# A graph layer and a feed-forward layer on one core: the node pass written out straight, its up product in three single-pass products, its first statistics on ScalarE, and smaller rings in the edge pass

## The reference

```python
def reference(x, src, dst, W, attn_l, attn_r, W_res, W1, b1, W2, b2, ...):
    h = layernorm(x)
    hv = h.reshape(n, 12, 64)
    ft = einsum('nhd,od->nho', hv, W)                  # per head, one 64x64 matrix
    e = leaky_relu(sum(ft * attn_l)[src] + sum(ft * attn_r)[dst], 0.2)
    alpha = segment_softmax(e, dst)
    agg = segment_sum(alpha[:, :, None] * ft[src], dst, n)
    res = einsum('nhd,od->nho', hv, W_res)
    x = x + relu(agg + res)
    t = layernorm(x)
    # rows 6 and up: one hidden layer of 96; the first 6 rows: pairs of experts and a gate
    x = x + concat(class_rows(t[:6]), gelu(t[6:] @ W1 + b1) @ W2 + b2)
    return x
```

## Time and profile before

| | us |
|---|---|
| median of three runs | 3060.57 |
| the profiled execution, its own time | 3053.38 |
| its span, first to last instruction | 3051.6 |
| TensorE busy | 2867.4 (94%) |
| VectorE busy | 2484.8 (81%) |
| GpSimd busy | 2140.6 (70%) |
| ScalarE busy | 1829.4 (60%) |

### The profile page before, as it was taken

The page is one execution under the profiler, slowest core; times in us unless marked ns, Lnnn a source line. Parts: engine busy times, 40 slices in busy tenths (PEclk is TensorE's granted clock), DMA queues, the critical chain, the costliest instruction groups (busy, mean ns, idle before and its releaser), DMA issues. The chain is left out here.

```text
span 3051.6 us, 69396 instructions
## 1 busy us (share of the span) xinstructions
PE 2867.4 (94%) x20124; PEld 2554.1 (84%) x20124; DVE 2484.8 (81%) x5828; ACT 1829.4 (60%) x3384; POOL 2140.6 (70%) x2027
## 2 busy tenths in 40 slices
PE   2999999999999984799999999999999999999998
PEld 2988888888888863688888888898988989889896
DVE  4799999999999964688878787787877888778883
ACT  1666666666666631566666666666666666666662
POOL 6766666666666500778877787787877878778782
PEclk9999999999999995799999999999999999999998
DMA  7999999988888624799988888888888888888873
GB/s 180 203 223 217 215 214 224 214 218 218 217 216 217 175 90 156 237 325 315 317 287 309 272 300 286 287 298 287 295 286 276 299 275 301 272 276 295 277 253 122
DMA packets 246672, 758.47 MB, mean 249 GB/s; under 512 B 78899, under 2 KB 81203, under 8 KB 246291
## 3 DMA queue, kind: packets, MB, share of 16 engines
q1 hardware_dynamic: 176644, 545.08, 50.4%
q0 software_dynamic: 69312, 209.33, 30.4%
q10 hardware_dynamic: 432, 0.62, 0.1%
HBM read 623.04 MB, written 232.17 MB: 280 GB/s over the span
## 5 line engine op out<-in xcount | busy, mean ns | idle before, releaser
L647 ACT ACTIVATE arena<-ps 128x768 f32<-128x768 f32 x392 | 317.3, 810 | 550.1 <-PE ps L707 550.0
L860 PE MATMUL ps<-wr_bd,arena 128*128 128x128 f32 x4704 | 600.3, 278 | 35.2 <-DVE arena L1179 34.1
L860 PEld LDWEIGHTS ps<-wr_bd,arena 128*128 128x128 f32 x4704 | 565.6, 194 | 43.2 <-issue 34.8
L839 PE MATMUL ps<-arena,w_sb 128*96 128x256 f32 x2352 | 580.6, 383 | 0.0
L570 POOL DMA_INDIRECT arena<-agg_scratch,nrow x392 | 438.9, 1120 | 78.1 <-issue 69.8
L1174 DVE SCALAR_TENSOR_TENSOR ps<-ps,r_n,arena 128x768 f32<-128x768 f32 x392 | 400.1, 1021 | 54.1 <-DMA arena<-agg_scratch,nrow 32.5
L839 PEld LDWEIGHTS ps<-arena,w_sb 128*96 128x96 f32 x2352 | 368.0, 165 | 85.9
L550 POOL TENSOR_SCALAR arena<-csr_neg,mv,r_n 128x768 f32<-128x768 f32 x392 | 385.9, 984 | 52.4 <-POOL r_n L578 42.1
L609 ACT ACTIVATE arena<-ps 128x512 f32<-128x512 f32 x588 | 307.5, 594 | 189.9 <-PE ps L724 188.5
L1163 DVE TENSOR_TENSOR arena<-arena,ps 128x768 f32<-128x768 f32 x392 | 363.7, 928 | 53.3 <-issue 36.5
L1179 DVE SCALAR_TENSOR_TENSOR arena<-ps,arena 128x768 f32<-128x768 f32 x392 | 375.4, 958 | 17.1
(11 more groups left out here) (197 smaller groups left out, 5420.0 us busy)
## 6 DMA issues: line engine op xcount, KB each, us to landing
arena<-in_x SPq DMA_DIRECT2D x196, 768.0 KB, 6.2
arena<-in_x_cols SPq DMA_DIRECT2D x392, 384.0 KB, 4.7
out<-arena SPq DMA_DIRECT2D x195, 768.0 KB, 5.2
agg_scratch<-arena SPq DMA_DIRECT2D x196, 384.0 KB, 6.4
arena<-in_x,e_slot POOLq DMA_INDIRECT x392, 6.5
arena<-agg_scratch,nrow POOLq DMA_INDIRECT x392, 6.2
row_scratch<-e_slot POOLq DMA_INDIRECT x196
nrow<-row_scratch SPq DMA_DIRECT2D x196, 1.0 KB, 7.1
```

The lines of the kernel that those rows point to most:

```text
L839: last = nc.tensor.matmul(ps[0:HID, 6 + v, 0:PAIR * P], w1_sb[:, i, :], t2[:, v, i, :], start=(i == 0), stop=(i == NC - 1))
L860: last = nc.tensor.matmul(pair(1)[:, i * P:(i + 1) * P], xt_ring[:, g, i * P:(i + 1) * P], wr_bd[:], start=True, stop=True)
```

## The change

- Node pass: `U` becomes 196, so the 392 units are two blocks, both written out, and `turns` makes no loop.
- Up product: w1 is split once into w1_hi and w1_lo (float32r). ScalarE's copy writes t2_hi; VectorE makes t2_lo, transposes less t2_hi, in each unit, after L1179 and ahead of ve_n. L839 becomes three products for each of the three before. The next unit's transposes wait for t2_lo and not for the copy.
- First norm: bn_stats and bn_aggr on VectorE and their small operation go; ScalarE makes sum and square for both tiles of a pair, in every unit, linked by one semaphore s_st1.
- Edge pass: the transpose of dst_slot and the comparison move from 9 to 20 chunks behind (`L_DT`), after the transposes of the rows in TensorE's order; the mask ring has 2 places. dst_slot and same_x are copied 15 behind, ahead of the two norm steps of VectorE. `agg_ring` has 2 places (`AR`).
- The copy for the class rows reads PSUM; w1_sb and v_sb move into the arena.

```diff
-U = 28
+U = 196
+AR = 2
+L_DT = 20
@@ turns
-    with eng.Fori(2, n) as b:
-        yield b
+    if n > 2:
+        with eng.Fori(2, n) as b:
+            yield b
@@ tensors
-        mask_ring = part(32424, BODY, P)
-        both_t = part(34216, 2, 2 * D)
-        agg_ring = part(37544, G, D)
+        mask_ring = part(32424, 2, P)
+        both_t = part(32680, 2, 2 * D)
+        agg_ring = part(35752, AR, D)
-        t2 = part(38400, 2, NC, PAIR * P)
+        w1_hi = sb("w1_hi", [P, NC, HID], f32r)
+        w1_lo = sb("w1_lo", [P, NC, HID], f32r)
+        t2_hi = sb("t2_hi", [P, 2, NC, PAIR * P], f32r)
+        t2_lo = sb("t2_lo", [P, 2, NC, PAIR * P], f32r)
@@ ScalarE, node pass
-                    if u % PAIR == 0 and exists(ts, NT):
+                    if exists(ts, NT):
...
-                        act.wait_ge(s_sum1, b * (U // PAIR) + (u - 1) // PAIR + 1)
-                        nc.scalar.activation(junk[:, 0, :], x_ring[:, v, :], ACT.Square, bias=mv1[:, w, 2:3],
-                                             scale=-1.0, accum_out=q_st[:, w, 0:1]).then_inc(s_sq1, 1)
+                        act.wait_ge(s_st1, 2 * t - 1)
+                        nc.scalar.activation(junk[:, 0, :], x_ring[:, v, :], ACT.Square, bias=mv1[:, w, 2 * k:2 * k + 1],
+                                             scale=-1.0, accum_out=q_st[:, w, k:k + 1]).then_inc(s_st1, 1)
...
-                        nc.scalar.activation(t2[:, v, :, k * P:(k + 1) * P], pair(0).rearrange("p (c n) -> p c n", c=NC),
-                                             ACT.Copy).then_inc(s_te2, 1)
+                        nc.scalar.activation(t2_hi[:, v, :, k * P:(k + 1) * P],
+                                             pair(0).rearrange("p (c n) -> p c n", c=NC), ACT.Copy).then_inc(s_te2, 1)
...
-                    if u % PAIR == 1 and exists(t, NT):
+                    if exists(t, NT):
...
-                        at_least(act, s_sq1, b * (U // PAIR) + u // PAIR)
+                        at_least(act, s_st1, 2 * t)
                         at_least(act, s_base, t - XR + 1)
                         nc.scalar.activation(junk[:, 0, :], x_ring[:, v, :], ACT.Copy, scale=1.0 / D,
-                                             accum_out=mv1[:, w, 2:3])\
-                            .then_inc(s_sum1, 1)
+                                             accum_out=mv1[:, w, 2 * k:2 * k + 1])\
+                            .then_inc(s_st1, 1)
@@ TensorE, edge pass
-                    if exists(ct, EC + 1):
-                        at_least(pe, s_mask, ct)
+                    cd = c - L_DT
+                    if exists(cd, EC + 1):
+                        at_least(pe, s_mask, cd)
...
+                    if exists(cd, EC):
+                        v = (i - L_DT) % BODY
+                        pe.wait_ge(s_dsl, 2 * b + (i - L_DT) // G + 1)
+                        nc.tensor.transpose(dst_ps, dst_slot[:, v // G, v % G:v % G + 1].to_broadcast([P, P]), ident[:])\
+                            .then_inc(s_tds, 1)
@@ TensorE, node pass
-                        at_least(pe, s_te2, tt)
+                        at_least(pe, s_lo2, tt)
                         transposes(pair(0), n2[:, (u - L_T2) % 2, :], s_tp2)
...
-                            pe.wait_ge(s_te2, tu + PAIR)
+                            pe.wait_ge(s_lo2, tu + PAIR)
...
-                            last = nc.tensor.matmul(ps[0:HID, 6 + v, 0:PAIR * P], w1_sb[:, i, :], t2[:, v, i, :],
-                                                    start=(i == 0), stop=(i == NC - 1))
+                            for n, (w, h) in enumerate(((w1_hi, t2_hi[:, v]), (w1_lo, t2_hi[:, v]), (w1_hi, t2_lo[:, v]))):
+                                last = nc.tensor.matmul(ps[0:HID, 6 + v, 0:PAIR * P], w[:, i, :], h[:, i, :],
+                                                        start=(i == 0 and n == 0), stop=(i == NC - 1 and n == 2))
@@ VectorE, setup
+            link_up(V.tensor_copy(w1_hi[:], w1_sb))
+            V.tensor_tensor(w1_lo[:], w1_sb, w1_hi[:].bitcast(f32), ALU.subtract)
@@ VectorE, edge pass
+                    gc = 2 * b + (i - 15) // G
+                    if k == 1 and exists(gc, NG):
+                        w = (i - 15) // G % 2
+                        at_least(dve, s_ert, gc - 1)
+                        at_least(dve, s_tds, G * (gc - 1))
+                        V.tensor_copy(dst_slot[:, w, :], dstbf[:, ds(G * gc, G)])
...
-                        at_least(dve, d_agg[j], 16 * (2 * b + (i - L_AGG) // G))
-                        V.scalar_tensor_tensor(agg_ring[:, j, :].rearrange("p (c f) -> p c f", f=P),
+                        at_least(dve, d_agg[v % AR], 16 * (BODY // AR * b + (i - L_AGG) // AR))
+                        V.scalar_tensor_tensor(agg_ring[:, v % AR, :].rearrange("p (c f) -> p c f", f=P),
...
-                    if exists(ct, EC):
-                        v = (i - L_TR) % BODY
+                    cd = c - L_DT
+                    if exists(cd, EC):
+                        v = (i - L_DT) % BODY
                         w, j = v // G, v % G
-                        dve.wait_ge(s_tds, ct + 1)
-                        at_least(dve, s_sum, ct - BODY + 1)
-                        V.tensor_scalar(mask_ring[:, v, :], dst_ps, dst_slot[:, w, j:j + 1], None,
+                        dve.wait_ge(s_tds, cd + 1)
+                        at_least(dve, s_sum, cd - 1)
+                        V.tensor_scalar(mask_ring[:, v % 2, :], dst_ps, dst_slot[:, w, j:j + 1], None,
                                         ALU.is_equal).then_inc(s_mask, 1)
@@ VectorE, node pass
+                    tl = t - L_T2
+                    if exists(tl, NT):
+                        v, k = (u - L_T2) // PAIR % 2, (u - L_T2) % PAIR
+                        f = slice(k * P, (k + 1) * P)
+                        dve.wait_ge(s_te2, tl + 1)
+                        V.tensor_tensor(t2_lo[:, v, :, f], pair(0).rearrange("p (c n) -> p c n", c=NC),
+                                        t2_hi[:, v, :, f].bitcast(f32), ALU.subtract).then_inc(s_lo2, 1)
...
-                        V.tensor_scalar(ve_n[:, w, 0:1], mv1[:, w, 1:2], EPS, None, ALU.add)
-                        V.tensor_scalar(ve_n[:, w, 1:2], q_st[:, w, 0:1], 1.0 / D, EPS, ALU.mult, ALU.add)
+                        V.tensor_scalar(ve_n[:, w, 0:2], q_st[:, w, 0:2], 1.0 / D, EPS, ALU.mult, ALU.add)
...
-                        for h in range(2):
-                            V.bn_stats(bn1[:, u // PAIR % 2, h, :], x_ring[:, v, h * (D // 2):(h + 1) * (D // 2)]).then_inc(s_bn1, 1)
...
-                        V.bn_aggr(mv1[:, w, 0:2], bn1[:, u // PAIR % 2, :, :].rearrange("p a b -> p (a b)")).then_inc(s_ag1, 1)
```

More of the change, by code:

```diff
@@ L146, in gnn_ffn_kernel @@
         n2 = part(32256, 2, D)
-        t2 = part(38400, 2, NC, PAIR * P)
         junk = part(35328, 2, D)
-        cls_x = part(36864, PAIR, D, rows=NCLS // PAIR)
+        cls_x = part(33792, PAIR, D, rows=NCLS // PAIR)
         a1_sb = part(0, NC, NEXP, HID)
@@ L169, in gnn_ffn_kernel @@
         fix_rows = part(25364, 2, D, rows=EH)
-        pens = part(34216, 2, EC, rows=HEADS)
-        m_run = part(34608, EC + 1, rows=HEADS)
-        t_run = part(34806, EC + 1, rows=HEADS)
-        gap = part(35004, 4, EC, rows=HEADS)
-        coef = part(35788, 4, EC, rows=HEADS)
+        pens = part(32680, 2, EC, rows=HEADS)
+        m_run = part(33072, EC + 1, rows=HEADS)
+        t_run = part(33270, EC + 1, rows=HEADS)
+        gap = part(33468, 4, EC, rows=HEADS)
+        coef = part(34252, 4, EC, rows=HEADS)
         w2_sb = part(21504, D, rows=HID + 1)
+        w1_sb = part(24000, NC, HID)
+        v_sb = part(24600, NC * (2 * HEADS + 2))
         w_dup = part(22272, P, rows=DH)
@@ L321, in gnn_ffn_kernel @@
         s_eo = sem("s_eo")
-        d_agg = [sem(f"d_agg{u}") for u in range(G)]
+        d_agg = [sem(f"d_agg{u}") for u in range(AR)]
         d_tab = sem("d_tab")
@@ L342, in gnn_ffn_kernel @@
         d_g = [sem(f"d_g{u}") for u in range(GR)]
-        s_bn1 = sem("s_bn1")
-        s_ag1 = sem("s_ag1")
-        s_sum1 = sem("s_sum1")
-        s_sq1 = sem("s_sq1")
+        s_st1 = sem("s_st1")
+        s_lo2 = sem("s_lo2")
         s_ven = sem("s_ven")
@@ L430, in _ @@
                              tab_d[k * HEADS:(k + 1) * HEADS]).then_inc(l_tab, 16)
-            for u in range(G):
-                sp.wait_ge(d_agg[u], 16 * (EC // G))
+            for u in range(AR):
+                sp.wait_ge(d_agg[u], 16 * (EC // AR))
             sp.dma_start(o_last, tail_v[:, :, P - 1, :]).then_inc(d_last, 16)
@@ L524, in _ @@
                             .then_inc(s_rpd, 1)
-            for u in range(G):
-                pool.wait_ge(d_agg[u], 16 * (EC // G))
+            for u in range(AR):
+                pool.wait_ge(d_agg[u], 16 * (EC // AR))
             pool.wait_ge(s_idx, 1)
@@ L646, in _ @@
                         at_least(act, s_up, b * (U // PAIR) + (u - L_T2) // PAIR - 1)
[L647 to L648 removed]
```

(17 more changed lines are left out.)

63 lines of the change are left out of this document (23 added, 40 removed).

## The result

The changed kernel takes 3024.85 us (median of four runs, 3022.7 to 3033.3) against 3061.51 for the kernel before: ratio 0.9889 [0.9864, 0.9913], 37 us less. The forecast was 74 less. The profiled execution takes 3026.7 us, not 2980, so 47 us have to be found.

The account below looks back on a forecast made before the run. TensorE was taken to bound the kernel, with a gather loop hidden just under it. Straight line -54, node-pass unit -27 and edge pass +8 made -73: profiled 3053.4 to 2980, 7 more for the median, 2987 us; range 2905 to 3075.

Parts of the forecast that it names:

- Straight line, -54: Node pass: writing out both turns removes the loop's instruction waits and low clock, 54 us less.
- TensorE's unit 4.08: Node pass: nine single-pass up products cut TensorE's work per unit from 4.34 to 4.08 us, -102 if all counts.
- VectorE 7.86 a pair: Node pass: t2_lo added and bn work removed take VectorE from 7.43 to 7.86 us a pair, 3.93 a unit.
- The unit T = 4.27, -27 us: Node pass: the odd gather's landing sets the unit at 4.27 us, between bounds 4.08 and 4.50, gaining 27 us.
- 2T = 1.30 + L - 0.86: Node pass: two units span store to gather use, with L the odd gather's landing after the store, 8.1; T = 4.27.
- the one the prediction first wrote: Node pass: loop from ve_n through power, base and odd gather to ve_n two pairs on, 4.30 us a unit before.
- store + 8.1: Node pass: the odd gather lands 8.1 us after the store, when store and the load behind it are through.
- The edge pass, +8: Edge pass: the output ring of two makes chunks wait for stores, between 0 and 18 us, taken as +8.
- The mask's move at 0: Edge pass: moving the mask and its transpose from 9 to 20 chunks behind costs 0.
- The clock: Node pass: TensorE keeps the full clock despite idling some 0.2 us a unit, so nothing was put down.
- Rival 1: Node pass: TensorE stays the bound, the late gather taken up, T = 4.08, -152 us, 2908 us; chance 0.25.
- Rivals 3 and 4: Node pass, gather landing L from issue: 3, L 7.7 to 7.9, about no change, 0.15; 4, 8.1 or more, slower, 0.18.

Follow-up runs that it names:

- the two sides: Kernel before with the node pass written out without a loop, 3013.50 us; changed kernel with the loop put back, 3064.90 us.
- experiment 5: Changed kernel with ve_n put ahead of t2_lo in VectorE's order: 2987.98 us.
- experiments 6 and 7: Changed kernel: 6 with only the even tile of each pair stored, 2953.95 us; 7 with the load of x issued away from the store, 2945.52 us.
- experiment 2: Kernel before with U of 196, so the node pass has no loop, and nothing else: 3013.50 us.
- experiments 1 and 9: 1: kernel before, output ring of two, 3075.56 us; 9: kernel before, mask moved, 3061.87, plus ring of two, 3064.61; changed kernel, ring of three, 3006.97.
- experiment 4: Changed kernel with the up product again in fp32, without w1_hi, w1_lo and t2_lo: 3019.39 us.
- experiment 8: Changed kernel with ve_n ahead of t2_lo and, on GpSimd, each gather issued ahead of n2: 3128.41 us.

## Why the prediction came out wrong

**Direction, and the range of 2905 to 3075, held; the size of the gain did not.** Step by step:

- *Straight line, -54.* Right in kind, a little large: 40 to 50 from the two sides, no "issue" wait of a turn left, and no price for straight code.
- *TensorE's unit 4.08.* Right: 4.10, products at 0.11 to 0.12. As forecast it no longer decides.
- *VectorE 7.86 a pair.* The pair without a late gather is 2013.62 - 2005.48 = 8.14, so 4.07 a unit: h_lo's 0.16 of waiting is in it, and the rest are small differences in start-to-start times. VectorE's busy share of 1279.6 / 1400 = 91% is the forecast 92%. ScalarE: 1247.9 of 1400 at 4.36 is 3.89 a unit (3.95 forecast).
- *The unit T = 4.27, -27 us: the step that failed.* What it says of the wait holds: t2_lo delays ve_n (experiment 5), and the odd gather's data are tied to the burst of store and load, not to its issue (experiments 6 and 7, and the packets). What failed is the balance 2T = 1.30 + L - 0.86, and the L in it.
  The balance takes the 0.86 from L1163 (now L1176) to L1174 (now L1187) as fixed. But the wait for the gather lies between these two: 2005.48 - 2003.66 = 1.82. L1176, and with it the next pair's store (2004.73), have gone ahead of the wait. What the late gather holds back is only the store after that, 2013.85 - 2005.48 = 8.37 us later. So the loop goes over two pairs, as the one the prediction first wrote did: 4T = 9.23 + 8.37 = 17.60, which is 2013.85 - 1996.25. Over the 80 late odd gathers the medians are 9.03 and 8.35, so T = 17.38 / 4 = 4.35, beside 4.36 measured. This also tells why about every second pair escapes (from one late odd gather to the next it is two pairs in 53 of 79 cases): the L1187 of 2013.62 comes 8.89 after its store, because the late one before it has already moved it. This working is from the trace; no run was made to test it.
  The L: "store + 8.1" was one gather's landing, while 1304.75 to 1313.87 in the earlier trace rows was 9.12.
  The two errors partly cancel. The balance with 9.03 gives 4.73, the loop of two pairs with 8.1 gives 4.11. That 4.27 came out within 0.09 of the measured 4.36 is luck.
  What counts is the gain, and it was small because the loop stood level with TensorE already: in experiment 2, where TensorE still has its 4.34, the 68 late odd gathers have medians of 8.76 and 8.61, which is 4.34 too. From that 4.388 to 4.360 it is 11 us instead of 27.
- *The edge pass, +8.* Mis-sized, and at the edge of its bounds: by medians 10, 4 and 18 us (experiments 1 and 9), in the profiled execution 31.4 us of waits for stores, which I bounded at 18. The bound held the landings of the kernel before as fixed; what they are with two places no trace shows. Why the ring costs 18 us in the changed kernel and 4 to 10 in the kernel before is open: the tensors' places in SBUF and two more copies in the setup also differ, and no run parts them. The mask's move at 0 was right.
- *The execution that the sum started from.* Its edge pass began some 11 us quicker than that of experiments 2 and 9, which moves the profiled start of the node pass, not the medians. The changed kernel's was the slowest of the seven with its edge pass. With the ring's waits it makes the 34 us: about 11 + 19 in the first 300 us, the rest later.
- *The clock.* In the node pass it stayed at 1.00 with TensorE 96% busy, as forecast. In the first part of the edge pass it did not, below.

By medians: -40 to -55 for the line, +4 to +18 for the ring, and for the rest of the node pass between -11 (the profiles of experiment 2 and the changed kernel) and +5 (3024.85 against 3019.39 in experiment 4). That is -62 to -17, with -37 measured, and -27 to -42 by its interval. How the 13 to 18 us between experiment 2 and the changed kernel divide between the ring and the node pass, the medians don't settle.

Rival 1 was right that TensorE and VectorE could go at about 4.1 and wrong that the gather would pass the burst. Rivals 3 and 4 counted L from the issue; the 7.70 from issue to use is in 3's span, but only because the issue came later in a burst that didn't move.

## What to carry to other kernels

When a cut makes the busiest engine lighter by 6%, look first at which transfer the next engine waits for, and what else is issued in the two microseconds around it: here moving a 768 KB load by 4 us gave 65 us in the node pass, more than the 37 of the whole change. Size such a wait from issue or burst to *use* over many units, not from one landing. When you write a loop's balance, look which side of the wait each step of it stands on: a step ahead of the wait isn't held back by it. And take an early, noisy stretch of a profile from more than one execution before you subtract from it.

## What the runs showed of the hardware

- The odd gather is used 9.12 us after the store when issued with it (before) and 9.23 when issued 1.53 later (changed); with the load 4 us away from the store it is mostly in time. From 1998 to 2002 us, right behind its issue, 292 packets of SyncE's queue start and none of GpSimd's.
- A gather directly behind the base in GpSimd's order stands idle 0.85 to 1.13 us before it starts, with n2 between them 0.17 (experiment 8).
- A late store costs more than its wait, through the clock. L1005 waited 5.45 us until 171.50, TensorE's sum behind it 4.39 until 172.56, and TensorE's granted clock went from 1.00 to 0.53, near the lower of its two levels, 1.2 instead of 2.4 GHz. The table of the changed kernel:

```profile
162.00:166.00 4.00, 3.52 (x25) 2.88 (x25) 3.90 (x11) 2.48 (x5) 2.16 (x2) 1.00 1.17 169
166.00:170.00 4.00, 2.17 (x21) 2.07 (x19) 0.04 (x1) 1.03 (x2) 3.35 (x4) 1.00 0.99 253
170.00:174.00 4.00, 1.44 (x2) 0.83 (x3) 2.50 (x4) 0.00 (x0) 0.19 (x1) 0.61 0.97 166
174.00:178.00 4.00, 4.00 (x17) 3.28 (x16) 3.04 (x12) 1.41 (x2) 1.63 (x2) 0.53 0.61 213
```
